# A gated four-layer stack on one core: cross attention in double steps, local heads turned later, and weight loads in another order

## The chip, the cores and the metric

One Trainium2 chip, one core of it. The metric is the time of one execution on the device in microseconds; the runs of the kernel before gave a median of 3140.57 us.

## The reference, cut to what matters

The whole program takes 2 sequences of 1024 tokens of width 256 (2048 tokens, held as 16 tiles of 128) through four layers of gated attention and gated feed-forward blocks. Two parts of it matter here.

The cross attention of layer 1 (16 heads of 64, keys from a context of 154 tokens), without its layer norm:

```python
q = (xn @ w_q).reshape(B, SQ, H, DH)
k, v = jnp.split(context @ w_kv, 2, axis=-1)
p = softmax(q @ k.T * DH ** -0.5)
x = x + tanh(g) * tanh(gate) * ((p @ v) @ w_out + b_out)
```

The local block of layer 2, run twice (DEPTH = 2), each time windowed attention (8 heads of 64, windows of 128 that look one window back) and then a gated feed-forward network:

```python
x1, x2 = split(h, 2); h = concat([x1, shift(x2, 1)])
q, k, v = split(h @ wqkv, 3)
q, k = l2norm(q) * q_scale, l2norm(k) * k_scale
q, k = rotary_xpos(q, k)
y = y + local_attention(q, k, v) @ wo
h = layernorm(shift_token(y)) * g + b
a, gate = split(h @ w1 + b1, 2)
y = y + (a * gelu(gate)) @ w2 + b2
```

Products in full precision are made of three passes over an "upper" and a "rest" part of each factor (`three`, `products`).

## The kernel before, in words

`gated_layers` runs the blocks one after the other. Each block is a function that hands each engine its own list of instructions, written out by hand in the order of the Python loops, with semaphores between the engines; nothing reorders them. Every `with nc.Block()` ends in a barrier of all engines, the small ones in `Weights` too: `Weights.__init__` issues the DMA of a pack of weights on SyncE, and `need()` makes SyncE wait until it landed, which holds all engines at the barrier.

**Cross attention** (`cross_attention`, second half, L1221 on). The unit of work u is one group of 512 tokens (4 tiles) by 4 heads: 4 groups by 4 quads, 16 units. A step n is one tile of a unit, 4 steps to a unit (64 in all). For a step TensorE makes the scores into one of two pairs of PSUM banks, VectorE takes the row's least (`largest`, L1411; the scores are negated), ScalarE four exponentials with their sums (`exps`, L1355), VectorE inverts the sums (`invert`, L1416), GpSimd multiplies (L1391), TensorE turns the probabilities two steps later (`turn_probs`), VectorE copies them out (`take_turned`, L1423), and with the last tile also the tails (L1426). For each unit TensorE also makes the queries of the next one in two halves (`project_q`, bank `QB`), which ScalarE and VectorE copy out in an upper and a rest part (`take_q` L1345, `rest_q` L1430), and the weighted values of the unit before in two halves (`weighted`, L1301 and L1305, bank `OB`), copied out the same way (`take_o` L1365, `rest_o`, recorded at the helper's line L164). After each fourth unit the output projection (`project_out`) runs in two halves through the same bank `OB`, and `add_y` (L1444) adds it to x. So `QB` and `OB` hold one item each, and the second half of a unit's weighted values waits until the first was copied out.

**Local heads** (`local_heads`), once per layer and sequence, four times in all, 8 tiles each. TensorE makes q, k and v of a tile (`qkv`, 18 matmuls), ScalarE squares q and k (L1718), VectorE sums the squares (L1749) and makes the products with the rotation tables (L1759 to L1761) and, once ScalarE took the roots (L1734), clamps and inverts them (L1764, L1766); GpSimd adds the two products (L1794) and multiplies by the inverse (L1798). One tile later TensorE turns the result (`turn_heads`, L1693), and ScalarE (L1725, L1728) and VectorE (L1771, L164) copy it out. `c_part` and `s_part` have two slots each.

**Local attention** (`local_attend`): two steps per tile (4 heads each); ScalarE and VectorE copy out the turned probabilities (`take_own` L1901, `take_prev` L1946) and each second step the weighted values (`take_o` L1907, `rest_o` L164).

**Local feed-forward** (`local_ffn`): `w.need()`, then `shifted_norm`, then `feed_forward`. Of the pack `L2f` the norm uses only the gain and shift, in ScalarE's last pass (L1582). For the second layer the packs are issued in the order L2r, L2a (the attention's, needed after the feed-forward) and L2f (the feed-forward's own).

## Time and profile before

| what | us |
|---|---|
| runs, median of 3 (lowest to highest) | 3140.57 (3138.81 to 3149.53) |
| the profiled execution, its own time | 3145.08 |
| its span, first to last instruction | 3143.3 |
| cross attention, main loop, in the span | about 985 to 1283 |
| the four runs of local heads | start at 1865.0, 2013.2, 2327.3 and 2477.7 |
| local heads, first run | 1864.9 to 1935 |
| local attention behind it | 1935 to 2011 |
| feed-forward 1 of layer 2: first load issued, norm starts | 2160.77, 2177.34 |
| feed-forward 2 of layer 2: load issued, norm starts | 2628.35, 2637.18 |

The profile is of one execution. A timeline row has start, duration, engine, line, operation, what it writes from what it reads, how many instructions it merges, and in brackets how long the engine had been idle before it and what released it. PE is TensorE, PEld its weight loads, DVE VectorE, ACT ScalarE, POOL GpSimd, SPq the queue of SyncE. The kernel is a long chain of blocks with barriers between them, so a block that ends earlier moves all that follows.

### The profile page before, as it was taken

What the parts mean: (1) busy time and instruction counts of PE and PEld (TensorE: products, weight loads), DVE (VectorE), ACT (ScalarE), POOL (GpSimd) and SP (SyncE); (2) the same over time, 40 slices, a digit from 0 to 9 for tenths busy, and PEclk for the clock granted to TensorE, in tenths of its full rate; (3) what the DMA queues carried; (4) which work ended last, traced back from release to release, by engine and by line L of the source; (5) the groups of instructions that cost most, each with busy time, mean ns of one, the idle gap of its engine ahead of it and who ended that gap; (6) DMA issues with size and microseconds to landing.
All of it is one profiled execution on the core that took longest, in us unless ns stands there. A gap on an engine that the chain in (4) does not pass through costs nothing. (4 is left out here: it accounts for less than half of the span.)

```text
span 3143.3 us, 42991 instructions
## 1 busy us (share of the span) xinstructions
PE 2438.3 (78%) x15657; PEld 1661.7 (53%) x15716; DVE 2007.2 (64%) x4265; ACT 1253.9 (40%) x2974; POOL 937.5 (30%) x867
## 2 busy tenths in 40 slices
PE   6799999979997898499997757775977776961254
PEld 3233333347876665378884446654866665850122
DVE  4588888725666555467764446565556565569898
ACT  4366666623434444143331115453334453320121
POOL 2000000004544333055550015351434442422343
PEclk9799999988998999789997679998988987985566
DMA  1111111010000000200000010001000000010000
GB/s 68 22 29 29 28 28 27 20 63 1 1 21 36 1 1 1 104 1 1 1 1 24 1 45 1 1 1 76 1 1 1 1 1 30 1 41 0 0 1 27
DMA packets 15681, 57.90 MB, mean 18 GB/s; under 512 B 7408, under 2 KB 7408, under 8 KB 13552
## 3 DMA queue, kind: packets, MB, share of 16 engines
q1 hardware_dynamic: 15472, 55.15, 5.3%
q8 instruction: 126, 2.06, 0.3%
q14 instruction: 83, 0.68, 0.1%
HBM read 39.37 MB, written 2.10 MB: 13 GB/s over the span
## 5 line engine op out<-in xcount | busy, mean ns | idle before, releaser
L2267 ACT ACTIVATE probs<-psum 128x512 f32<-128x512 f32 (+1 forms) x640 | 346.7, 593 | 195.8 <-PE psum L2211 194.9
L2282 DVE TENSOR_REDUCE max_parts<-psum 128x1 f32<-128x512 f32 x512 | 328.7, 685 | 63.2 <-PE psum L2184 59.5
L152 PE MATMUL psum<-x_upper,weights_upper 128*128 128x512 f32 (+2 forms) x624 | 252.9, 405 | 26.0 <-POOL weights_rest L164 17.0
L152 PE MATMUL psum<-x_rest,weights_upper 128*128 128x512 f32 (+2 forms) x624 | 249.7, 400 | 0.0
L152 PE MATMUL psum<-x_upper,weights_rest 128*128 128x512 f32 (+2 forms) x624 | 247.3, 396 | 0.0
L152 PE MATMUL psum<-weights_upper,hidden_upper 128*128 128x256 f32 (+2 forms) x768 | 242.3, 316 | 1.8 <-DVE x_tok L311 1.7
L164 POOL TENSOR_TENSOR weights_rest<-L1f,weights_upper 128x256 fp32r<-128x256 f32 x216 | 181.4, 866 | 183.8 <-ACT weights_upper L269 183.8
L152 PE MATMUL psum<-weights_upper,hidden_rest 128*128 128x256 f32 (+2 forms) x768 | 217.4, 283 | 0.0
L152 PE MATMUL psum<-weights_rest,hidden_upper 128*128 128x256 f32 (+2 forms) x768 | 217.2, 283 | 0.0
L2222 PE MATMUL psum<-probs,v_tok 128*17 128x256 f32 (+1 forms) x2560 | 201.1, 385 | 0.4 <-ACT probs L2267 0.4
L2211 PE MATMUL psum<-q_stack,k_stack 98*128 98x512 bf16 (+1 forms) x640 | 198.2, 387 | 0.5
L2432 POOL MEMSET selectors<- 128x2048 bf16 x1 | 1.8, 1805 | 611.1 <-DVEq L2429 611.1
L164 DVE TENSOR_TENSOR hidden_rest<-hidden,hidden_upper 128x512 fp32r<-128x512 f32 x192 | 170.3, 887 | 6.6
L2184 PE MATMUL psum<-k_stack,q_stack 96*128 96x512 bf16 x512 | 160.3, 393 | 14.9 <-DMA k_stack<-k_parts 14.9
L1921 POOL TENSOR_TENSOR probs<-probs,row_sum 128x1024 f32<-128x1024 f32 x64 | 120.9, 1894 | 165.6 <-DVE row_sum L1940 165.6
L1893 ACT ACTIVATE probs<-probs,row_least 128x256 f32<-128x256 f32 x256 | 126.9, 497 | 87.2 <-DVE row_least L1934 87.2
L164 POOL TENSOR_TENSOR weights_rest<-L2f,weights_upper 128x256 fp32r<-128x256 f32 (+1 forms) x144 | 101.6, 735 | 193.9 <-ACT weights_upper L269 193.9
L152 PEld LDWEIGHTS psum<-weights_upper,hidden_upper 128*128 128x128 f32 (+2 forms) x768 | 147.5, 192 | 12.9 <-issue 6.7
L152 PEld LDWEIGHTS psum<-weights_rest,hidden_upper 128*128 128x128 f32 (+2 forms) x768 | 146.8, 191 | 4.6
L164 POOL TENSOR_TENSOR weights_rest<-L0f,weights_upper 128x256 fp32r<-128x256 f32 x128 | 106.1, 849 | 141.7 <-ACT weights_upper L269 141.7
L152 PEld LDWEIGHTS psum<-weights_upper,hidden_rest 128*128 128x128 f32 (+2 forms) x768 | 146.5, 191 | 0.0
L152 PEld LDWEIGHTS psum<-x_upper,weights_upper 128*128 128x128 f32 (+2 forms) x624 | 117.9, 189 | 50.8 <-issue 18.1
(432 smaller groups left out, 6075.7 us busy)
## 6 DMA issues: line engine op xcount, KB each, us to landing
L1f<-in_L1f SPq DMA_DIRECT2D x1, 7936.0 KB, 21.5
k_stack<-k_parts SPq DMA_DIRECT2D x192, 36.8 KB, 2.0
q_stack<-q_parts SPq DMA_DIRECT2D x192, 32.0 KB, 2.0
L0f<-in_L0f SPq DMA_DIRECT2D x1, 4760.0 KB, 14.2
L2f<-in_L2f SPq DMA_DIRECT2D x2, 2268.0 KB, 11.6
L1x<-in_L1x SPq DMA_DIRECT2D x1, 4226.0 KB, 13.0
L2a<-in_L2a SPq DMA_DIRECT2D x2, 2048.0 KB, 10.0
L3f<-in_L3f SPq DMA_DIRECT2D x1, 3072.0 KB, 10.4
```

Source lines behind the costliest of these rows:

```text
L152: ins = pe.matmul(out, lhsT(a).bitcast(F32R), rhs(b).bitcast(F32R), start=start and n == 0, stop=stop and n == len(PASSES) - 1, skip_group ...
L164: return engine.tensor_tensor(dst.bitcast(F32R), src, up_part, ALU.subtract)
L1893: ins = act.activation(pb[:, n % NPB, h, :], pb[:, n % NPB, h, :], ACT.Exp, bias=mn[:, n % NPB, h:h + 1], scale=-1.0, accum_out=sm[:, n % ...
L1921: pool.tensor_tensor(pb[:, n % NPB], pb[:, n % NPB], spread(sm[:, n % NPB, :], 2 * P), ALU.mult)\
L2184: pe.matmul(net.ps[:, XB + (2 * n + k) % 3, :], lhsT, ks[0:ROWS, s, k * 512:(k + 1) * 512], start=True, stop=True).then_inc(x_done, 1)
L2211: pe.matmul(net.ps[0:m, STB + hf, :], ks[0:ROWS + 2, s, k * P:k * P + m], qs[0:ROWS + 2, s, hf * 512:(hf + 1) * 512], start=True, stop=True)\
L2222: ins = pe.matmul(net.ps[32 * j:32 * j + HD + 1, PVB + u % 2, 0:256], vt[0:m, b, k, h, :], pb[0:m, n % NPB, j * 256:(j + 1) * 256], start= ...
L2267: act.activation(pb[0:m, s % NPB, hf * 512:(hf + 1) * 512], net.ps[0:m, STB + hf, :], ACT.Exp, scale=HD ** -0.5).then_inc(exp_done, 1)
L2282: v.tensor_reduce(mx3[:, u % 2, q, k:k + 1], net.ps[:, XB + (2 * n + k) % 3, :], AX.X, ALU.max).then_inc(x_taken, 1)
L2432: pool.memset(sel[:], 0.0)
```

## The change: what it does

Five edits.

1. Cross attention: the banks `QB` and `OB` become a ring of two banks that all items (halves of queries, of weighted values, of projections) enter in the order of the list `ring`; an item waits until the one two places earlier was copied out (`enter`). One counter `made`, one `item_upper` and one `taken` replace those of each kind.
2. Cross attention goes in double steps: two steps' scores, a turn, the query half, (a projection half), a turn, and each second time both halves of the weighted values together. ScalarE does two steps' exponentials in a row and copies both halves of the weighted values at the head of a unit; VectorE's order follows. `exps` gets four slots, the query pair three half slots, the tails one slot.
3. Local heads: tiles are turned two tiles later (`LAG`), with a third slot of `c_part`; `s_part` keeps two and gets a wait of its own on `added`.
4. Local attention: ScalarE copies the turned probabilities before the weighted values, and VectorE too.
5. Local feed-forward: `need()` comes behind the norm, whose ScalarE waits for the pack before its last pass. In the second layer L2f is issued first, then L2a, then L2r.

```diff
-            NE, NPB = 3, 2
+            NE, NPB = 4, 2
             U = G * QUADS
-            N = U * GT
-            SLOT, TB, TAILB, OB, QB = 0, 4, 5, 6, 7
+            DU = 2 * U
+            SLOT, TB, TAILB, RING = 0, 4, 5, 6
...
-            tT = net.sb(ctx, "tailsT", [P, 2, GN])
-            qT = two(ctx, "q_pair", [P, 2, 2, GN])
+            tT = net.sb(ctx, "tailsT", [P, GN])
+            qT = two(ctx, "q_pair", [P, 3, GN])
...
+            y_unit = lambda u: u >= 2 and (u - 2) % QUADS == QUADS - 1
+            ring = [("q", 0, 0), ("q", 0, 1)]
+            for u in range(U + 2):
+                for d in range(2):
+                    if u + 1 < U:
+                        ring.append(("q", u + 1, d))
+                    if y_unit(u):
+                        ring.append(("y", group(u - 2), d))
+                    if d == 1 and 1 <= u <= U:
+                        ring += [("o", u - 1, 0), ("o", u - 1, 1)]
+            place = {item: n for n, item in enumerate(ring)}
+            uppers = {item: n for n, item in enumerate(i for i in ring if i[0] != "y")}
+            qslot = lambda u, a: (2 * u + a) % 3
+            bank = lambda item: net.ps[:, RING + place[item] % 2, :]
...
+                def enter(item):
+                    if place[item] >= 2:
+                        pe.wait_ge(taken, place[item] - 1)
...
-                    i, g, hp = 2 * u + a, group(u), (u % QUADS) * 2 + a
-                    if i >= 1:
-                        pe.wait_ge(q_ready, i)
+                    g, hp = group(u), (u % QUADS) * 2 + a
+                    enter(("q", u, a))
...
-                        ins = three(pe, net.ps[:, QB, :], [p[:, c, hp * P:(hp + 1) * P] for p in wq],
+                        ins = three(pe, bank(("q", u, a)), [p[:, c, hp * P:(hp + 1) * P] for p in wq],
...
                     pe.wait_ge(tails_taken, u + 1)
-                    if i >= 1:
-                        pe.wait_ge(o_taken, i)
-                    if y_items(u + 2):
-                        pe.wait_ge(y_taken, y_items(u + 2))
+                    enter(("o", u, a))
+                    out = bank(("o", u, a))
...
                 pe.wait_ge(cleared, 1)
                 for a in range(2):
                     project_q(0, a)
-                for n in range(N + 2 * GT):
-                    u, j = divmod(n, GT)
-                    if n < N:
-                        scores(n)
-                    if j % 2 == 0 and u + 1 < U:
-                        project_q(u + 1, j // 2)
-                    if j < 2 and y_due(u):
-                        project_out(u, j)
-                    if 2 <= n < N + 2:
-                        turn_probs(n - 2)
-                    if j >= 2 and 1 <= u <= U:
-                        weighted(u - 1, j - 2)
+                for u in range(U + 2):
+                    for d in range(2):
+                        for j in (2 * d, 2 * d + 1):
+                            if u < U:
+                                scores(u * GT + j)
+                        before = u * GT + 2 * d - 2
+                        if 0 <= before < U * GT:
+                            turn_probs(before)
+                        if u + 1 < U:
+                            project_q(u + 1, d)
+                        if y_unit(u):
+                            project_out(group(u - 2), d)
+                        if 0 <= before < U * GT:
+                            turn_probs(before + 1)
+                        if d == 1 and 1 <= u <= U:
+                            weighted(u - 1, 0)
+                            weighted(u - 1, 1)
...
-                    i = 2 * u + a
-                    act.wait_ge(pv_done, i + 1)
-                    if u % QUADS == 0 and a == 0 and u > 0:
-                        act.wait_ge(projected, y_items(u + 2))
-                    act.copy(oT[0][:, (u % QUADS) * 2 + a, :].bitcast(F32R), net.ps[:, OB, :]).then_inc(o_upper, 1)
+                    act.wait_ge(made, place["o", u, a] + 1)
+                    act.copy(oT[0][:, (u % QUADS) * 2 + a, :].bitcast(F32R), bank(("o", u, a))).then_inc(item_upper, 1)
...
-                for n in range(N + 2 * GT):
-                    u, j = divmod(n, GT)
-                    if j == 3 and 1 <= u <= U:
-                        take_o(u - 1, 0)
-                    if j == 0 and 2 <= u <= U + 1:
-                        take_o(u - 2, 1)
-                    if n < N:
-                        exps(n)
-                    if j % 2 == 0 and u + 1 < U:
-                        take_q(u + 1, j // 2)
+                for u in range(U + 2):
+                    for d in range(2):
+                        if d == 0 and 2 <= u <= U + 1:
+                            take_o(u - 2, 0)
+                            take_o(u - 2, 1)
+                        for j in (2 * d, 2 * d + 1):
+                            if u < U:
+                                exps(u * GT + j)
+                        if u + 1 < U:
+                            if d == 1:
+                                act.wait_ge(s_done, 2 * GT * (u + 1))
+                            take_q(u + 1, d)
...
+                        if u >= 1:
+                            v.wait_ge(made, place["o", u - 1, 1] + 1)
+                        v.tensor_copy(tT[:], net.ps[:, TAILB, :]).then_inc(tails_taken, 1)
...
-                for n in range(N + 2 * GT):
-                    u, j = divmod(n, GT)
-                    if n < N:
-                        largest(n)
-                    if 1 <= n <= N:
-                        invert(n - 1)
-                    if j % 2 == 1 and u + 1 < U:
-                        rest_q(u + 1, j // 2)
-                    if j == 3 and 1 <= u <= U:
-                        rest_o(u - 1, 0)
-                    if j == 0 and 2 <= u <= U + 1:
-                        rest_o(u - 2, 1)
-                    if 2 <= n < N + 2:
-                        take_turned(n - 2)
-                    if j < 2 and y_due(u):
-                        add_y(u, j)
-                    if j == 2 and u % QUADS == 1 and group(u) + 1 < G:
-                        g = group(u) + 1
-                        if g >= 2:
-                            v.wait_ge(q_made, 2 * QUADS * (g - 1))
-                        upper(v, xg[0][:, g % 2], whole_x(g)).then_inc(x_upper, 1)
+                for u in range(U + 2):
+                    for d in range(2):
+                        n = u * GT + 2 * d
+                        if n < U * GT:
+                            largest(n)
+                        if d == 0 and 2 <= u <= U + 1:
+                            rest_o(u - 2, 0)
+                        if n < U * GT:
+                            largest(n + 1)
+                        if d == 0 and 2 <= u <= U + 1:
+                            rest_o(u - 2, 1)
+                        if 2 <= n < U * GT + 2:
+                            take_turned(n - 2)
+                        if n < U * GT:
+                            invert(n)
+                        if 2 <= n < U * GT + 2:
+                            take_turned(n - 1)
+                        if u + 1 < U:
+                            rest_q(u + 1, d)
+                        if y_unit(u):
+                            add_y(group(u - 2), d)
+                        if n < U * GT:
+                            invert(n + 1)
+                        if d == 1 and u % QUADS == 1 and group(u) + 1 < G:
+                            g = group(u) + 1
+                            if g >= 2:
+                                v.wait_ge(made, place["q", (g - 1) * QUADS - 1, 1] + 1)
+                            upper(v, xg[0][:, g % 2], whole_x(g)).then_inc(x_upper, 1)
...
+            act.wait_ge(after.landed, 16)
...
-    NB = 2
+    NB, NSP, LAG = 3, 2, 2
...
-        s_part = net.sb(ctx, "sin_part", [P, NB, 2, HD])
...
-            for t in range(WIN + 1):
+            for t in range(WIN + LAG):
                 if t < WIN:
                     qkv(t)
-                if t >= 1:
-                    turn_heads(t - 1)
+                if t >= LAG:
+                    turn_heads(t - LAG)
...
-                if t >= 1:
-                    k = t - 1
+                if t >= LAG:
+                    k = t - LAG
...
+                if t >= NSP:
+                    v.wait_ge(added, t - NSP + 1)
...
-                    sp_ = s_part[:, t % NB, n].rearrange("p (h d) -> p h d", d=LD)
+                    sp_ = s_part[:, t % NSP, n].rearrange("p (h d) -> p h d", d=LD)
...
-                if t >= 1:
-                    take_rest(t - 1)
+                if t >= LAG:
+                    take_rest(t - LAG)
...
                     exps(n)
+                if 2 <= n < N + 2:
+                    take_own(n - 2)
                 if n >= 4 and n % 2 == 0 and (n - 4) // 2 < WIN:
                     take_o((n - 4) // 2)
-                if 2 <= n < N + 2:
-                    take_own(n - 2)
...
                     invert(n - 1)
+                if 2 <= n < N + 2:
+                    take_prev(n - 2)
                 if n >= 4 and n % 2 == 0 and (n - 4) // 2 < WIN:
                     rest_o((n - 4) // 2)
-                if 2 <= n < N + 2:
-                    take_prev(n - 2)
...
+        shifted_norm(net, y, hT, w("gain"), w("shift"), w)
         w.need()
-        shifted_norm(net, y, hT, w("gain"), w("shift"))
...
+        if load:
+            self.load()
+
+    def load(self):
+        with self.net.nc.Block() as block:
             @block.sync
             def _(sp):
-                sp.dma_start(memory[:], dram).then_inc(self.landed, 16)
+                sp.dma_start(self.memory[:], self.dram).then_inc(self.landed, 16)
...
-                lw = LocalWeights(net, sub, 1)
+                lw = LocalWeights(net, sub, 1, load=False)
                 with ExitStack() as ffn:
-                    local_ffn(net, y, Weights(net, ffn, "L2f0"))
+                    w = Weights(net, ffn, "L2f0")
+                    lw.pack.load()
+                    lw.rot.load()
+                    local_ffn(net, y, w)
```

**VectorE in cross attention, one unit in the middle.** Before (one unit without a projection; probsT is `take_turned`, tailsT its tails, oT_rest `rest_o`, row_least `largest`, row_sum `invert`):

```order
L1423 COPY probsT<-psum 128x4x128
L1411 TENSOR_REDUCE row_least<-psum 128x4
L1416 RECIPROCAL row_sum<-row_sum 128x4
L1430 SCALAR_TENSOR_TENSOR q_pair_rest<-psum,q_pair_upper 128x512
L164 TENSOR_TENSOR oT_rest<-psum,oT_upper 128x512
L1423 COPY probsT<-psum 128x4x128
L1411 TENSOR_REDUCE row_least<-psum 128x4
L1416 RECIPROCAL row_sum<-row_sum 128x4
L164 TENSOR_TENSOR oT_rest<-psum,oT_upper 128x512
L1423 COPY probsT<-psum 128x4x128
L1411 TENSOR_REDUCE row_least<-psum 128x4
L1416 RECIPROCAL row_sum<-row_sum 128x4
```

The change:

```order
L1419 TENSOR_REDUCE row_least<-psum 128x4 x2
L1431 COPY probsT<-psum 128x4x128
L1424 RECIPROCAL row_sum<-row_sum 128x4
L1431 COPY probsT<-psum 128x4x128
L1440 SCALAR_TENSOR_TENSOR q_pair_rest<-psum,q_pair_upper 128x512
L1424 RECIPROCAL row_sum<-row_sum 128x4
L1419 TENSOR_REDUCE row_least<-psum 128x4
L164 TENSOR_TENSOR oT_rest<-psum,oT_upper 128x512
L1419 TENSOR_REDUCE row_least<-psum 128x4
L164 TENSOR_TENSOR oT_rest<-psum,oT_upper 128x512
L1431 COPY probsT<-psum 128x4x128
L1424 RECIPROCAL row_sum<-row_sum 128x4
```

Two row_least now stand in a row, both oT_rest stand at the head of the unit, each behind one row_least, and each pair of probsT has a row_sum between them.

**ScalarE at the head of a local heads run** (squares are of tile 0, 1, 2; qT_upper and keysT_upper copy out a turned tile). Before:

```order
L1718 ACTIVATE squares<-psum 128x1024
L1732 COPY values<-psum 128x512
L1734 ACTIVATE norms<-norms 128x16
L1718 ACTIVATE squares<-psum 128x1024
L1725 ACTIVATE qT_upper<-psum 128x4x128
L1728 CAST keysT_upper<-psum 128x4x128
L1732 COPY values<-psum 128x512
L1734 ACTIVATE norms<-norms 128x16
L1718 ACTIVATE squares<-psum 128x1024
```

The change:

```order
L1735 ACTIVATE squares<-psum 128x1024
L1749 COPY values<-psum 128x512
L1751 ACTIVATE norms<-norms 128x16
L1735 ACTIVATE squares<-psum 128x1024
L1749 COPY values<-psum 128x512
L1751 ACTIVATE norms<-norms 128x16
L1735 ACTIVATE squares<-psum 128x1024
L1742 ACTIVATE qT_upper<-psum 128x4x128
L1745 CAST keysT_upper<-psum 128x4x128
```

The first copies of a turned tile have moved from behind the second squares to behind the third; TensorE's first turn has moved in the same way, from ahead of the third tile's 18 matmuls to behind them.

## Rows read from the trace of the kernel before

**Rows 1.** Stretches: length, busy us (xcount) of PE PEld DVE ACT POOL, PEclk, DMA share, GB/s

```profile
985.00:1285.00 300.00, 257.89 (x1918) 180.31 (x1916) 151.42 (x283) 137.84 (x577) 105.04 (x136) 0.98 0.01 3
1865.00:1935.00 70.00, 49.53 (x224) 39.91 (x224) 47.89 (x94) 24.42 (x44) 34.20 (x16) 0.87 0.00 1
```

**Rows 2.** Waits in 985:1285: us in total, times, longest us

```profile
PE psum L1301 <- DVE oT_rest L164: 25.9, 16, 1.7
```

**Rows 3.** Timeline of VectorE in cross attention: tails of units 0, 5, 6, 15, last add

```profile
1005.70 0.68 DVE L1426 COPY tailsT<-psum 128x512 f32<-128x512 f32 x1
...
1090.41 0.68 DVE L1426 COPY tailsT<-psum 128x512 f32<-128x512 f32 x1
...
1105.00 0.68 DVE L1426 COPY tailsT<-psum 128x512 f32<-128x512 f32 x1
...
1261.30 0.68 DVE L1426 COPY tailsT<-psum 128x512 f32<-128x512 f32 x1
...
1281.64 0.75 DVE L1444 SCALAR_TENSOR_TENSOR x_tok<-psum,cross_factor,x_tok 128x512 f32<-128x512 f32 x1 [6.02 <-PE psum L1089]
```

**Rows 4.** Timeline of all engines in cross attention, start of unit 6

```profile
1084.50 0.19 PEld L1272 LDWEIGHTS psum<-keys_upper,q_pair_upper 64*128 64x128 f32 x2 [0.81 <-issue]
...
1085.33 0.19 PEld L1089 LDWEIGHTS psum<-x_group_upper,wq_upper 128*128 128x128 f32 x1
...
1086.31 0.39 ACT L1355 ACTIVATE exps<-psum,row_least 128x154 f32<-128x154 f32 x1 [1.11 <-DVE row_least L1411]
...
1086.84 0.60 PE L1287 MATMUL psum<-const,probs 128*128 128x128 f32 x4
...
1087.79 0.61 ACT L1345 ACTIVATE q_pair_upper<-psum 128x512 fp32r<-128x512 f32 x1
...
1092.09 1.08 PE L1301 MATMUL psum<-probsT,values 128*64 128x512 f32 x4
...
1093.95 0.19 PEld L1272 LDWEIGHTS psum<-keys_upper,q_pair_upper 64*128 64x128 f32 x2 [0.81 <-ACT exps L1355]
```

**Rows 5.** Timeline of VectorE in local heads: first run, last two rows third run

```profile
1880.03 1.22 DVE L1749 TENSOR_REDUCE norms<-squares 128x16 f32<-128x1024 f32 x1
...
1890.73 1.22 DVE L1749 TENSOR_REDUCE norms<-squares 128x16 f32<-128x1024 f32 x1 [1.74 <-ACT squares L1718]
...
1895.90 1.21 DVE L1749 TENSOR_REDUCE norms<-squares 128x16 f32<-128x1024 f32 x1
...
1914.57 1.15 DVE L1764 TENSOR_SCALAR norms<-norms 128x16 f32<-128x16 f32 x1 [1.36 <-ACT norms L1734]
...
1923.05 1.22 DVE L1749 TENSOR_REDUCE norms<-squares 128x16 f32<-128x1024 f32 x1 [0.69 <-ACT squares L1718]
...
1934.25 0.69 DVE L164 TENSOR_TENSOR keysT_rest<-psum,keysT_upper 128x512 fp32r<-128x512 f32 x1
...
2351.31 1.22 DVE L1749 TENSOR_REDUCE norms<-squares 128x16 f32<-128x1024 f32 x1 [1.90 <-ACT squares L1718]
...
2387.22 1.21 DVE L1749 TENSOR_REDUCE norms<-squares 128x16 f32<-128x1024 f32 x1
```

**Rows 6.** Timeline of ScalarE and TensorE in local attention, an even step

```profile
1968.82 0.56 ACT L1907 CAST oT_upper<-psum 128x512 fp32r<-128x512 f32 x1
...
1970.81 1.09 PE L1864 MATMUL psum<-probsT,values 128*64 128x128 f32 x16 [1.55 <-DVE probsT L1946]
```

**Rows 7.** Timeline of the first local feed-forward: loads, norm's start, ScalarE's last pass

```profile
2160.77 0.33 SPq L2365 DMA_DIRECT2D L2r<-in_L2r  x1
2161.49 0.33 SPq L2365 DMA_DIRECT2D L2a<-in_L2a  x1
...
2177.44 0.22 DVE L1539 MEMSET stats<- 128x192 f32 x1 [17.82 <-PEq L2368]
...
2188.47 0.78 ACT L1582 ACTIVATE hT<-psum,L2f 128x512 f32<-128x512 f32 x1 [2.76 <-PE psum L1527]
```

**Rows 8.** DMA issues in 2625:2640: line, form, KB, us from issue to landing

```profile
L2f<-in_L2f SPq DMA_DIRECT2D x1, 2268.0 KB, 8.4
```

More of the change, by code:

```diff
@@ L1599, in __init__ @@
         self.pack_scope = ctx.enter_context(ExitStack())
-        self.pack = Weights(net, self.pack_scope, f"L2a{layer}")
+        self.pack = Weights(net, self.pack_scope, f"L2a{layer}", load)
     def split(self, net):
@@ L1711, in _ @@
                         .then_inc(h_upper, 1)
-            for t in range(WIN + 1):
+            for t in range(WIN + LAG):
                 if t < WIN:
```

89 lines of the change are left out of this document (38 added, 51 removed).

## Prediction

> **What bounds the kernel now.** I read the stretches first, then the waits of the stretch in question, then the timeline. In cross attention's main loop TensorE is busy 257.9 of 300 us at a granted clock of 0.98, with VectorE, ScalarE and GpSimd at half or less [rows 1]: TensorE is the bound there, and what can be won is its idle time. The waits name the largest piece: 16 times, once a unit, it waits up to 1.7 us for VectorE's copy of the first half of the weighted values, 25.9 us in all [rows 2]. A unit takes 14.59 us from tails to tails [rows 3]. In the first local heads run no engine is full: TensorE 49.5, VectorE 47.9 of 70 us [rows 1]. VectorE's timeline tells why: a tile begins with L1749, and the starts are 10.7 us apart from tile 1 to 2, then 5.17 us to tile 3 with no idle time noted, and 27.15 us for the four tiles to tile 7 [rows 5]. So a tile costs VectorE 5.17 us, and the rest is waiting on a loop through GpSimd and the turn. In the third run the five tiles from 2 to 7 take 35.91 us [rows 5]. In the first feed-forward of layer 2's local block the norm starts 16.7 us after the first load was issued, and ScalarE touches the pack only 11.0 us after that [rows 7].
>
> **The change part by part.** *Loads.* Before, the norm starts at 2177.44. Now it starts when three loads are issued, 0.72 us apart [rows 7]: 2160.77 + 3 x 0.72 = 2162.9, 14.5 us earlier. ScalarE's last pass would come at 2162.9 + 11.0 = 2173.9. L2f, now first on SyncE's queue, needs 8.4 us alone [rows 8], so it is there by 2169.2, 4.7 us ahead; if the three packs shared the engines evenly, they would land where they do now, just before 2177.4, and 3.5 us of the gain were lost. L2a and L2r land beside the norm and are wanted 160 us later. The second feed-forward has one load: 8.4 us from issue to landing less one empty step of 0.72 gives 7.7. `need()` stays as a block of its own, now exposed: 0.72 twice. Sum: 14.5 + 7.7 - 1.4 = **21 us off** (between 17 and 23).
>
> *Local heads.* Before, tile 2's matmuls wait behind the first turn, which waits for GpSimd. Now they follow tile 1 at once (their bank is free once VectorE made tile 0's products, before L1749 of tile 1 at 1880.03 [rows 5]). Two thirds of a tile's matmuls (about 2.8 us of its 5) and the squares put L1749 of tile 2 at 1884.4 instead of 1890.7. From there VectorE is the bound. I take 5.4 us a tile rather than 5.17, since TensorE's tile and turn fill almost as much. Tile 7 starts at 1884.4 + 5 x 5.4 = 1911.4 instead of 1923.05: 11.7 less. Behind it, a tail of 11.2 us to the last copy [rows 5] stays. The layout repeats in the second run. In the third, 4.4 + 27 = 31.4 us from tile 1 to 7 replace 10.7 (taken from the first run) + 35.9 = 46.6, 15.2 less, and the fourth I take alike. Sum: 2 x 11.7 + 2 x 15.2 = **54 us off**. At 5.17 a tile it is 58; at 6.0, 42; if only the start is won, 6.3 x 4 = 25.
>
> The third slot costs nothing: the wait for the turn of tile t-3 is over by then. `s_part` waits for GpSimd's sum of tile t-2, a tile old. ScalarE's root of tile t now stands behind copies of tile t-2, which wait for a turn that itself waits for VectorE's last copy; by the chain (a turn's first half 0.5, two copies and the values 1.5, the root 0.2, hand-overs 0.4) it is ready 2.7 us into VectorE's tile, and is wanted at 3.7.
>
> The clamp L1764 at 1914.57 took 1.15 us for 16 columns [rows 5]; it ran while GpSimd was at its sum, and reaches GpSimd more often now that GpSimd's 4.3 us a tile (34.2 us over 8 [rows 1]) must fit in 5.4 rather than 6.5. As the order stands, the clamp comes right behind the products, ahead of GpSimd's next sum. The Trainium skill, page "SBUF — State Buffer", section "Who interferes with whom", says that a tensor_scalar in a two-port mode and a GpSimd instruction exclude each other for the whole instruction, whoever issues first. By that rule the sum keeps its 54 us only as long as the clamp issues first; otherwise it is the rival on the clamp below.
>
> *Cross attention.* TensorE's own work in a unit: a step's scores 0.83, a query half 1.5, a turn 0.63 (these two from the remaining starts), half of the weighted values 1.86 [rows 4]: 4 x 0.83 + 2 x 1.5 + 4 x 0.63 + 2 x 1.86 = 12.6 of 14.6 us. The ring takes the 1.7 us away. What comes late next I step through from a unit's head, with 0.98 us from scores to exponentials, 1.48 for a step's exponentials [rows 4], and VectorE's copies at 0.6 to 0.68 [rows 3]. VectorE now does row_least, oT_rest, row_least, oT_rest before the first probsT, and has it done at 4.3; TensorE could turn the next at 3.8: 0.5 lost. The first query half waits 0.15 for oT_rest. The first probsT of the second double step stands behind two row_least: 0.35 lost. The second half of the weighted values shares a bank with the query half just made, whose copy stands on ScalarE behind two steps' exponentials, 2.96 us: 0.45 lost. Sum 1.45, so 14.1 us a unit, 0.45 less; 15 times, 6.5 us. A projection half enters between and keeps its length. The first unit has no weighted values to cover its query copy: the next unit's scores wait for both steps' exponentials, and I add 3 us. At the end, 20.3 us lie between the last tails and the last add [rows 3]; both halves of the weighted values and both of the projection now run without waiting for a copy of their bank: 1.7 + 1.1, and 2 more in the last units, which have no queries: 5 off. Sum: **8.5 us off**. Ends: TensorE without waits, 12.9 a unit, 15 x 1.7 = 25 off; 15.1 a unit, 8 more.
>
> *Local attention.* In even steps `take_own` goes ahead of `take_o`. The weighted values that follow at 1970.81 [rows 6] need both. VectorE's last copy then comes at the end of the same two copies of ScalarE, with its other copy already done: about 0.14 us less, 7 times a run; in the last even step 0.4 more. Four runs: **2 us off** (6 off to 4 on).
>
> **Sum.** 21 + 54 + 8.5 + 2 = 85.5 us off. On the profiled execution, 3145.1 - 85.5 = 3059.6; it lies 4.5 us above the median, so **3055 us** against 3140.6.
>
> **The rivals.** *Cross attention wins it all*: the waits I stepped through are in TensorE's queue slack; 17 us more off, 3038. For: the engines behind are half idle. Against: each is a real wait for a copy.
>
> *Cross attention loses a little*: double steps make each copy later; 8 us on instead of 8.5 off, 3072. For: three new waits of my own count. Against: 1.7 us are gone for certain.
>
> *Local heads keep their two speeds*: rest_out at the end of VectorE's tile holds the turn, the turn holds ScalarE's copies; only the starts are won, 29 us fewer, 3084. For: the turn still has one pair of banks. Against: the turn now has GpSimd's result a tile ahead, and that wait was the one seen.
>
> *The clamp waits for GpSimd*: if the root comes later than 3.7 us into the tile, GpSimd's sum has begun, and the clamp waits up to 2.4 us (the larger part of GpSimd's 4.3): 7.6 us a tile, 2 us on per run instead of 13.5 off, 62 us fewer, 3117. The page on SBUF, cited above, would make it so if GpSimd issued first. Against: a tile with the root in time shows VectorE's 5.17.
>
> *Slower, cross attention in series*: if a double step's probabilities must be through all engines before TensorE has anything to turn, it lasts 1.7 (scores) + 1.0 + 0.8 (row_least) + 3.0 (exponentials) + 0.3 + 2.8 (GpSimd) + 1.3 (turns) + 0.7 = 11.6 us, 23.2 a unit instead of 14.6: 16 x 8.6 = 138 on, less the other 77: 3201. It decides above 19.4 us a unit (14.6 + 77/16). Against: the turns of a double step are those of the double step before, so TensorE has half a unit of cover, 4 us and more.
>
> *The change doesn't do what it says*: the three packs land together and the norm's ScalarE waits: 3.5 us, within the range.
>
> **Numbers.** Forecast (3047 to 3064) 0.40; cross attention wins it all 0.15; loses a little 0.19; heads keep two speeds 0.14; the clamp 0.06; series 0.03; 0.03 for a mixture near no change (clamp and a small loss together with noise). The range runs from 3032 (heads at 5.17 and cross attention at 12.9) to 3090 (two speeds, with some of the loss) and leaves out about 0.15. A measurement of this kernel can tell 0.3%, 9.4 us, from no change. Faster by more: 0.94; within 0.03; slower 0.03.
>
> **What would show it.** In the profile of the changed kernel: the norms of layer 2's feed-forwards start right behind the issues, and ScalarE's L1582 group waits for TensorE, not for a DMA. Local heads: starts of the norms' reduction 5.2 to 5.5 us apart from tile 2 on, and the clamp at 0.17 us. Cross attention: tails 14.1 us apart, and the wait of the weighted values for oT_rest gone, with q_pair_rest in its place at some 0.5. Wrong would be: units above 14.6, a heads cadence that still alternates, clamps of over 1 us, or a ScalarE wait for L2f.

## The result and the profile after

The changed kernel takes **3063.58 us** (median of 4 runs, 3062.59 to 3064.13). The kernel before took 3139.69 us beside it; the ratio is 0.9752, with a 95% interval of 0.973 to 0.9774. Forecast were 3055, within 3032 to 3090. The profiled execution took 3064.06 us, its span is 3062.2 us and the mean granted clock 0.875 (before 0.876).

Stretches, in us, from the two profiled executions. Local heads are counted from the first clearing of hT to the first masked scores of the attention, local attention from there to the next block's first event.

| stretch | before | after | forecast |
|---|---|---|---|
| cross attention, last addition at | 1281.64 | 1272.43, 9.2 less | 8.5 less |
| four runs of local heads | 289.3 | 235.0, 54.3 less | 54 less |
| four runs of local attention | 307.5 | 311.7, 4.2 more | 2 less |
| two feed-forwards with their loads | 323.8 | 301.7, 22.1 less | 21 less |
| whole time | 3145.08 | 3064.06, 81.0 less | 85.5 less |

Cross attention, VectorE's timeline: the tails of units 0, 5, 6 and 15 and the last addition (for [rows 3]).

```profile
1008.45 0.68 DVE L1436 COPY tailsT<-psum 128x512 f32<-128x512 f32 x1
...
1090.38 0.68 DVE L1436 COPY tailsT<-psum 128x512 f32<-128x512 f32 x1
...
1104.55 0.68 DVE L1436 COPY tailsT<-psum 128x512 f32<-128x512 f32 x1
...
1254.84 0.68 DVE L1436 COPY tailsT<-psum 128x512 f32<-128x512 f32 x1
...
1272.43 0.75 DVE L1453 SCALAR_TENSOR_TENSOR x_tok<-psum,cross_factor,x_tok 128x512 f32<-128x512 f32 x1 [4.94 <-PE psum L1089]
```

A unit takes 14.17 us (1104.55 less 1090.38) where it took 14.59. Its waits, in 975:1275 (us in total, times, longest), for [rows 2]:

```profile
PE psum L1299 <- DVE probsT L1431: 12.5, 22, 2.1
...
PE psum L1311 <- DVE q_pair_rest L1440: 8.2, 14, 1.5
...
PE psum L1089 <- DVE oT_rest L164: 3.5, 14, 1.5
```

The 25.9 us for `oT_rest` are gone. In their place stand three smaller waits, the three that the prediction had stepped through, 24.2 us together.

Local heads, second run: the starts of VectorE's reduction for tiles 0 to 3, then a clamp and the GpSimd instruction beside it (for [rows 5]).

```profile
2001.82 1.22 DVE L1766 TENSOR_REDUCE norms<-squares 128x16 f32<-128x1024 f32 x1 [5.70 <-ACT squares L1735]
2006.05 1.22 DVE L1766 TENSOR_REDUCE norms<-squares 128x16 f32<-128x1024 f32 x1
...
2010.27 1.16 DVE L1766 TENSOR_REDUCE norms<-squares 128x16 f32<-128x1024 f32 x1
2015.74 1.21 DVE L1766 TENSOR_REDUCE norms<-squares 128x16 f32<-128x1024 f32 x1
...
2034.88 0.17 DVE L1783 TENSOR_SCALAR norms<-norms 128x16 f32<-128x16 f32 x1
2035.05 2.40 POOL L1813 TENSOR_TENSOR cos_part<-cos_part,sin_part 128x1024 f32<-128x1024 f32 x1 [0.78 <-DVE sin_part L1780]
```

From tile 3 on the starts are 5.16 us apart (tile 7 starts at 2036.39). There the clamp takes 0.17 us and comes just ahead of GpSimd's sum; only in tiles 1 and 2 of each run does it take some 0.5 us.

Feed-forward 1 of layer 2 (for [rows 7]): the issues, the start of the norm, ScalarE's first pass over the pack.

```profile
2127.61 0.33 SPq L2388 DMA_DIRECT2D L2f<-in_L2f  x1
2128.34 0.33 SPq L2388 DMA_DIRECT2D L2a<-in_L2a  x1
2129.05 0.33 SPq L2388 DMA_DIRECT2D L2r<-in_L2r  x1
2129.90 0.22 DVE L1555 MEMSET stats<- 128x192 f32 x1 [3.43 <-PEq L2385]
...
2140.99 0.78 ACT L1599 ACTIVATE hT<-psum,L2f 128x512 f32<-128x512 f32 x1 [2.83 <-PE psum L1543]
```

The norm starts 2.3 us after the first issue instead of 16.7. ScalarE waits there for TensorE, not for a DMA.

### The profile page after: what moved, and what is told of

Same layout as the page of the kernel before. It is cut to its first block and busy times, and to the rows that moved or that the text cites. A ratio compares the mean times of both kernels' runs of the same rounds, so it can differ in the third digit from the quotient of the medians.

```text
span 3062.2 us, 43018 instructions
## 1 busy us (share of the span) xinstructions
PE 2434.4 (79%) x15716; PEld 1660.0 (54%) x15716; DVE 2003.3 (65%) x4265; ACT 1250.3 (41%) x2974; POOL 937.4 (31%) x867
## 5 line engine op out<-in xcount | busy, mean ns | idle before, releaser
L152 PE MATMUL psum<-x_upper,weights_upper 128*128 128x512 f32 (+2 forms) x624 | 253.1, 406 | 26.6 <-POOL weights_rest L164 17.6
L152 PEld LDWEIGHTS psum<-weights_upper,hidden_upper 128*128 128x128 f32 (+2 forms) x768 | 147.7, 192 | 12.8 <-issue 6.7
## 6 DMA issues: line engine op xcount, KB each, us to landing
L0f<-in_L0f SPq DMA_DIRECT2D x1, 4760.0 KB, 14.3
L1x<-in_L1x SPq DMA_DIRECT2D x1, 4226.0 KB, 13.1
```

The source lines that it names most:

```text
L152: ins = pe.matmul(out, lhsT(a).bitcast(F32R), rhs(b).bitcast(F32R), start=start and n == 0, stop=stop and n == len(PASSES) - 1, skip_group ...
```

## The experiments

### The four parts alone

Each is the kernel before with one part of the change: the new `local_heads`; the loads (`need`, the order of issues, the norm's wait); the new `cross_attention`; the order of the copies in `local_attend`, of which the cut below shows ScalarE's half (VectorE's `take_prev` and `rest_o` change places in the same way).

```
 kernel before, p1_heads          kernel before, p4_attend
-NB = 2                           -take_o((n - 4) // 2)
+NB, NSP, LAG = 3, 2, 2            take_own(n - 2)
...                               +take_o((n - 4) // 2)
```

> The kernel before with the new local heads alone. Theory: the four heads stretches lose 54 us as in the changed kernel, and the local attention stretches behind them grow by 1 to 1.8 us each although their own order is the old one, because TensorE comes out of the heads at the lower clock; so 48 to 51 us off in all. Rival (the new order of copies is what made local attention longer): attention stretches stay at 76.2 to 78.0 us and 54 us are off.

Measured: 3100.39 us, ratio 0.9864 (0.9849 to 0.9879), 42.4 off where 48 to 51 were expected. Heads 234.4 us in all, 54.8 less than in the trace before. Local attention 313.7 us, 6.2 more, **with the old order of copies**.

> The kernel before with the new loads and the norm's wait alone. Theory: 22 us off, 14.3 in the first feed-forward and 7.8 in the second, independent of the rest. Rival (part of it depends on the earlier end of the blocks ahead): under 18 us off.

Measured: 3126.90 us, 0.9951 (0.9935 to 0.9968). The feed-forwards are 13.7 and 7.5 us shorter, 21.2 in all. By the medians only 15.9 us are off, on the rival's side of 18. But the two stretches lost what the theory said, so the difference lies in stretches that this edit doesn't touch, such as the old cross loop, which ended 4.1 us later here than in the trace before.

> The kernel before with the new cross attention alone. Theory: 9 us off, units of 14.17 us. Rival (another stage pays for it through the clock): 9 us off inside the loop, less at the end of the program.

Measured: 3133.01 us, 0.9965 (0.995 to 0.9979). Units of 14.17 us, last addition at 1271.59.

> The kernel before with the new order of copies in local attention alone. Theory: pairs of steps 8.88 instead of 8.96 us, a few tenths lost at each run's end, so 0 to 2 us off, which timing can hardly tell from nothing. Rival (the order itself costs the 4.2 us by which the attention stretches grew): 3 to 5 us on.

Measured: 3140.76 us, 0.9994 (0.9984 to 1.0003). Local attention 307.1 us against 307.5.

What follows: the order of copies is worth nothing either way, and the attention's growth comes with the new heads. The four medians lie 42.4, 15.9, 9.8 and 2.0 us under the 3142.77 us of before in that series, 70 in all, where the whole change lies 76 under the kernel before in its own series (3139.69). The traces show part of why. The old code does not take the same time in every execution: the old cross loop ended at 1285.22, 1285.74 and 1282.62 in the traces with the heads, the loads and the order of copies alone, and at 1281.64 in the one read for the forecast. The old heads took 289.3 us in that one, but 287.1, 283.8 and 283.1 in the traces with the loads, the cross attention and the order of copies alone. Against 283 us the new heads win 49 and not 55, and with 6 to 7 us given back in the attention that is the 42.4 of the first run.

### TensorE's clock at the start of the attention

The granted clock of short stretches shows what the new heads do to the attention behind them. First before, then after, the fourth run: the 5 us from the first masked scores, and the next 5 (length, busy us of PE, PEld, DVE, ACT, POOL, PEclk, DMA share, GB/s).

```profile
2550.34:2555.34 5.00, 2.84 (x25) 2.35 (x23) 4.51 (x26) 4.53 (x19) 1.99 (x2) 0.72 0.02 3
2555.34:2560.34 5.00, 5.00 (x41) 4.28 (x42) 2.25 (x10) 3.97 (x16) 2.62 (x2) 0.66 0.00 0
```

```profile
2475.16:2480.16 5.00, 2.93 (x25) 2.34 (x23) 4.49 (x26) 4.53 (x19) 1.98 (x2) 0.50 0.00 0
2480.16:2485.16 5.00, 5.00 (x36) 4.45 (x36) 2.11 (x10) 2.89 (x12) 1.77 (x1) 0.50 0.00 0
```

0.50 is the lower level, 1.2 GHz. Run by run the attention grew by 1.1, 0.1, 1.8 and 1.2 us, and the second run, which did not grow, is the one where the clock reads as before. Its first 5 us, before and after:

```profile
2083.75:2088.75 5.00, 2.38 (x25) 1.88 (x23) 4.46 (x26) 4.53 (x19) 1.99 (x2) 0.82 0.01 2
```

```profile
2050.49:2055.49 5.00, 2.27 (x25) 1.77 (x23) 4.46 (x26) 4.53 (x19) 1.99 (x2) 0.84 0.00 2
```

In the new heads TensorE ends its projections early: it then has one group of eight transpositions left after 4.1 us of waiting and another after 1.5 us, and these already take 1.92 and 1.94 us where in mid-run they take 1.06 (second run, timeline after):

```profile
2041.79 1.92 PE L1710 MATMUL psum<-const,cos_part 128*128 128x128 f32 x8 [4.10 <-DVE keysT_rest L164]
...
2045.19 1.94 PE L1710 MATMUL psum<-const,cos_part 128*128 128x128 f32 x8 [1.49 <-DVE keysT_rest L164]
```

The kernel before ends its heads at the lower level too: its last group waits 5.17 us and takes 1.97 (first run).

```profile
1931.63 1.97 PE L1693 MATMUL psum<-const,cos_part 128*128 128x128 f32 x8 [5.17 <-POOL cos_part L1798]
```

What differs is how soon the clock comes back: there within the first 5 us of the attention, if not yet for good, after the change not before 10 us in three runs of four. Why it comes back later is not shown. The test keeps TensorE at work with matmuls whose results nobody reads:

```
+idle(14)                # 14 matmuls, 512 columns, free banks
 turn_heads(WIN - 2)
+idle(8)
 turn_heads(WIN - 1)
+idle(8)
...
 scores(2)               # in the attention: only in the second of these two kernels
+7 matmuls of 512 columns
 turn_probs(0)
```

> The changed kernel, with TensorE kept busy at the end of the local heads: 14 extra matmuls of 512 columns ahead of turning tile 6, 8 ahead of turning tile 7, 8 behind it, all into banks that nobody reads afterwards. Theory (the local attention is longer because TensorE enters it at 1.2 GHz, after about 4 us without work in the tail of the heads): the two last groups of eight turns take 1.1 us instead of 1.92, the tail of each run of heads is 1 to 1.5 us shorter, each stretch of local attention 1 to 1.5 us shorter and near the 76.2 to 78.0 us of the kernel before; in all 8 to 11 us, about 3054. Rival (something else at the start of the attention costs the time, e.g. what ScalarE and VectorE do there): stretches of attention stay at 77.1 to 79.2 us, and the extra matmuls cost nothing or hold up the turns by up to 1 us a run: 3063 to 3068.

Measured: 3048.62 us, 0.9703 (0.9688 to 0.9717). Heads 225.7 us, 9.3 less than after. Attention 310.2, only 1.5 less where 4 to 6 were expected.

> As the run before, and 7 more extra matmuls in the attention, ahead of its first transposition of probabilities, where TensorE waited 2.45 us for GpSimd. Theory: the first turned probabilities take 1.1 instead of 1.97 us, 1 us less a run than with the heads' extra matmuls alone: about 3050. Rival: the same time as the run before, or up to 1 us a run more, since the extra matmuls hold up that transposition.

Measured: 3044.02 us, 0.9686 (0.9672 to 0.9701), where 3050 was expected. Attention 302.7 us, 9.1 less than after and 7.5 less than in the run before, not 4. Heads 229.8, 4.1 more than in the run before: three of their four runs begin at a clock of 0.50 here, two there.

The same two windows of the fourth run, of the first and then of the second kernel:

```profile
2464.59:2469.59 5.00, 1.69 (x25) 1.27 (x21) 4.46 (x26) 4.76 (x20) 1.99 (x2) 0.85 0.00 0
2469.59:2474.59 5.00, 5.00 (x36) 4.45 (x36) 2.11 (x10) 2.89 (x12) 1.76 (x1) 0.50 0.01 3
```

```profile
2461.98:2466.98 5.00, 3.49 (x32) 2.51 (x28) 4.46 (x26) 4.76 (x20) 1.99 (x2) 1.00 0.01 3
2466.98:2471.98 5.00, 4.96 (x56) 4.07 (x56) 2.94 (x11) 4.46 (x17) 3.10 (x2) 1.00 0.00 0
```

So the clock is the cause of the attention's 4.2 us, and the theory was right on that and wrong on the place. Warm heads alone bring TensorE into the attention at 2.4 GHz, but it loses that again while it waits for GpSimd's first probabilities: the second window reads 0.50 in this fourth run and 0.66 in the other three. In those three the first output addition comes 24.5 us into the attention as in the kernel before (24.7), in this one at 25.4 as after the change, and with both waits filled at 23.1 in all four. Only with work in that wait too does the clock stay up, and the attention falls to 4.9 us less than in the kernel before.

### The clamp behind GpSimd's start

```
 ins.then_inc(parts, 1)          # GpSimd's sum may start
-v.wait_ge(sd_ready, t + 1)
-clamp, reciprocal
...
 take_rest(t - LAG)
+v.wait_ge(sd_ready, t + 1)
+clamp, reciprocal
```

> The changed kernel with the clamp and the reciprocal of the norms moved behind the taking of the tile before last, so that GpSimd's sum of 2.35 us has been running for about 1.3 us when the clamp comes. If the clamp must wait for a running GpSimd instruction: it takes about 1.1 us instead of 0.16 wherever it follows a taking, VectorE (which has some 0.1 us a tile to spare) falls behind by about 0.8 us a tile, 24 tiles: near 3080. If there is no such wait in this place: the clamp takes 0.16 us, 3063, within 0.2%.

Measured: 3083.89 us, 0.9815 (0.9799 to 0.9832), 20.3 us over the changed kernel; heads 257.6 us, 22.6 more. VectorE's group, then one tile of GpSimd and VectorE:

```profile
L1785 DVE TENSOR_SCALAR norms<-norms 128x16 f32<-128x16 f32 x32 | 36.4, 1137 | 0.0
```

```profile
2029.50 2.36 POOL L1817 TENSOR_TENSOR cos_part<-cos_part,sin_part 128x1024 f32<-128x1024 f32 x1 [1.62 <-DVE sin_part L1780]
...
2030.54 1.35 DVE L1785 TENSOR_SCALAR norms<-norms 128x16 f32<-128x16 f32 x1
```

The clamp begins 1.04 us into the sum and ends at 2031.89, with the sum (2031.86). The clamp of [rows 5] did the same in the kernel before: it ended at 1915.72, GpSimd's sum at 1915.68. So the rival on the clamp is a real mechanism. It didn't come because the root is ready in time and the clamp issues ahead of the sum. By the rule of the Trainium skill, page "SBUF — State Buffer", section "Who interferes with whom", which the prediction weighed, it is the one that issues first that keeps the other out; the trace agrees, 0.17 us when the clamp is first, 1.35 when the sum is.

### Slots or lag

```
-NB, NSP, LAG = 3, 2, 2
+NB, NSP, LAG = 3, 2, 1
```

> The changed kernel with three slots in the heads' cosine buffer, but turned one tile later, as before, instead of two. Theory (the lag is what took TensorE's wait for GpSimd away; slots alone only let VectorE run ahead): heads of 69 to 72 us instead of 58.7, 3063.6 plus 40 to 54, near 3110. Rival (VectorE's wait for a free slot was the tie): heads below 62 us, under 3075.

Measured: 3106.36 us, 0.9883 (0.9866 to 0.99); heads 283.8 us, as in the other traces with the old heads (283.1 to 289.3). TensorE's wait in the first run of heads is back, to the tenth what it was in the kernel before (second row):

```profile
PE psum L1710 <- POOL cos_part L1817: 17.6, 7, 5.2
```

```profile
PE psum L1693 <- POOL cos_part L1798: 17.6, 7, 5.2
```

It is the lag that gives the gain; the third slot alone gives nothing. Whether the lag would do without the third slot was not run. In this run local attention takes 307.1 us, so the old heads also bring back the old attention.

### Cross attention: the ring and the double steps

```
 for j in (2 * d, 2 * d + 1):
+    if u + 1 < U and j == 3:
+        act.wait_ge(s_done, 2 * GT * (u + 1))
+        take_q(u + 1, 1)
     exps(u * GT + j)
-if d == 1: ...take_q(u + 1, 1)
```

> The changed kernel, with ScalarE taking the unit's second projection between the third and the fourth list of exponentials instead of behind both (its wait for the scores still ahead of it). Theory (the unit of 14.17 us holds a wait of TensorE in front of the second weighted half for q_pair_rest, 14 times 0.58 us, because that projection is taken late): the wait L1311<-q_pair_rest goes, 0.4 us in each of 15 units, 5 to 6 us in all, about 3058. Rival: the fourth list of exponentials is now 0.6 us late, and what hangs on it (the reciprocal, GpSimd's share, the first scores of the next unit) takes the gain back: 3063, or up to 5 us more.

Measured: 3055.81 us, 0.9722 (0.9708 to 0.9737), 7.8 less than the changed kernel. Units of 13.54 and 13.78 us, last addition at 1263.72, 8.7 us earlier: 5 of it in the units and their end, as expected, and 3.7 in the first unit, whose tails now come at 1004.78. The fourth list's lateness took nothing back.

The next run keeps before's single steps and changes the banks. With them one copy moves: in the units with a projection VectorE takes the first query half ahead of the first addition, so that the ring's order holds.

```
-SLOT, TB, TAILB, OB, QB = 0, 4, 5, 6, 7
+SLOT, TB, TAILB, RING = 0, 4, 5, 6
+bank = lambda item: net.ps[:, RING + place[item] % 2, :]
```

> The changed kernel, with the cross attention of before in its single steps and its order, but with the ring of two banks in place of one bank for projections and one for outputs (in the units with a y, VectorE's taking of the first projection moved ahead of the first addition, so that the ring's order holds). Theory: the ring takes away the wait of the second weighted half for the first half's copy (25.9 us, 16 times 1.6), the double steps save little by themselves: last addition 6 to 9 us earlier than before's 1281.64, 3063 to 3067. Rival: it is the double steps that carry the gain, since in single steps the second half stands behind the copy of the projection instead: 3070 to 3074.

Measured: **3050.07 us**, 0.9704 (0.9684 to 0.9724), 13.5 less than the changed kernel. The theory said 3063 to 3067, the rival 3070 to 3074; both fell. Tails and the last addition:

```profile
1004.65 0.68 DVE L1431 COPY tailsT<-psum 128x512 f32<-128x512 f32 x1
...
1085.97 0.68 DVE L1431 COPY tailsT<-psum 128x512 f32<-128x512 f32 x1
...
1099.82 0.68 DVE L1431 COPY tailsT<-psum 128x512 f32<-128x512 f32 x1
...
1261.40 0.75 DVE L1449 SCALAR_TENSOR_TENSOR x_tok<-psum,cross_factor,x_tok 128x512 f32<-128x512 f32 x1 [4.85 <-PE psum L1089]
```

The tails are those of units 0, 5 and 6. A unit takes 13.85 us, the last addition comes 20.2 us earlier than before, and 11.0 earlier than after. So the ring alone is worth 20 us, and **the double steps, with their copies as ordered in this change, cost 11**. The first tails come at 1004.65 instead of 1008.45: 3.8 us in the first unit, where by the code the first query copy need no longer wait for both steps' exponentials. The next fourteen units take 229.0 instead of 231.8 us, and the last is 10.3 instead of 14.6; these last 4 us are the least certain, since in the traces of the run with a lag of 1 and of the first kernel of the next section, both in double steps, that unit took 10.7 too. Nor are the 11 us a price of double steps as such. The run with the early taking stays in double steps and won 8.7 us by the place of one copy of ScalarE, and the same loop in the first kernel of the next section ended at 1259.99, 1.4 us ahead of this one. TensorE's wait for `probsT` ahead of its turns (12.5 us after the change) is 1.4 us here, once. The largest that is left, in 975:1275:

```profile
PE psum L1311 <- DVE q_pair_rest L1435: 13.7, 14, 1.0
```

### A version that beats both

Two kernels put the pieces together. The first has the double steps with the early taking, and TensorE's extra matmuls at the end of the heads, in the attention and ahead of each run of heads:

```
+pe.wait_ge(qkv_upper, 3)        # while the weights are split
+20 matmuls of 512 columns
...
+6, 8 and 3 matmuls              # in the tail of local attention
```

> The changed kernel with three things together: ScalarE takes the second projection early in the cross attention; TensorE kept busy with extra matmuls at the end of the heads and ahead of the attention's first transposition; and, new, extra matmuls ahead of each run of heads too (20 while the local weights are split, 17 in three places of the tail of each local attention), since in the run with both warmings the heads still began at a granted clock of 0.50 where they took 58 us and at 1.00 where they took 55. From the run with both warmings (3044.0): minus 7.8 for the early taking, minus 3 for each of four runs of heads: 3024, if the pieces add up and the clock at the start of the heads is what separates 58 from 55. Rival: the start of the heads isn't set by the clock (VectorE and ScalarE move the first tiles): 3036. By either theory it is faster than both kernels.

Measured: 3032.83 us, 0.9649 (0.9632 to 0.9666). The pieces did not add up: the early taking and the attention kept theirs (last addition 1259.99, attention 302.6), but the heads won 5.2 us of 12. The first 8 us of the first and the second run of heads:

```profile
1844.47:1852.47 8.00, 6.02 (x27) 4.95 (x28) 2.57 (x6) 2.05 (x4) 0.00 (x0) 0.79 0.01 2
1976.26:1984.26 8.00, 6.02 (x34) 5.10 (x35) 2.58 (x7) 3.08 (x5) 0.00 (x0) 1.00 0.01 3
```

The second run, at 1.00, took 55.02 us; the other three began at 0.79 to 0.84 and took 56.4 to 56.6. The last kernel has the ring in single steps, VectorE's second taking one step earlier, and more extra matmuls where the clock was not yet up:

```
-if j == 3: rest_q(u + 1, 1)
+if j == 2: rest_q(u + 1, 1)     # at the step's end
...
-pe.wait_ge(qkv_upper, 3), 20 matmuls
+pe.wait_ge(qkv_upper, 1), 30 matmuls
...
+6 matmuls between turn_y and qkv(0)
```

> The ring in single steps (as in the run with the ring alone), with one more edit in it: VectorE takes the second projection at the end of step 2 instead of in step 3 behind the list and the reciprocal, since the trace of the ring alone shows TensorE's only regular wait of a unit there (the second weighted half for q_pair_rest, 14 times 0.98 us). Beside it the warmings of TensorE, with 30 instead of 20 extra matmuls at the splitting of the weights, and 6 between turning y and the first projection. From the kernel with all warmings and the early taking in double steps (3032.8, last addition at 1260): if the ring in single steps plus the earlier taking shortens a unit of 13.85 us by 0.7 to 0.9 in 15 units, the last addition comes at about 1249, and the time is near 3020, with up to 4 us less from the heads' starts. Rival: the unit is bound by TensorE's own work or by the lists of exponentials, and stays at 13.85: 3031 to 3034.

Measured: **3014.82 us** (5 runs, 3013.71 to 3015.45), 0.9596 (0.9583 to 0.9609) of the kernel before, 48.8 us under the changed kernel. Units take 12.8 us, the last addition comes at 1246.77, and TensorE's window is nearly full (first row); all four runs of heads start at 1.00 (second row, the first run) and take 55.0 us.

```profile
975.00:1242.00 267.00, 254.35 (x1905) 179.22 (x1904) 156.91 (x299) 137.10 (x577) 107.38 (x137) 0.99 0.01 1
```

```profile
1831.10:1839.10 8.00, 7.42 (x40) 6.13 (x41) 2.59 (x7) 3.09 (x5) 0.00 (x0) 1.00 0.00 0
```

## Why the prediction was right or wrong

**The direction and the likeliest case** held: 3063.6 lies in the forecast's own 3047 to 3064, if at its upper edge, and three of the four parts did what the prediction said they do. The sum was 4.5 us too large on the profiled execution (85.5 against 81.0). The median missed by 8.6 us, since the execution before lay 4.5 us above its median, and the one after only 0.5. Those 4.5 us sat mostly in the old heads: with the order of copies alone the profiled execution took 3139.15 us, 5.9 less than the one before, and its heads 6.2 less. So the forecast read its savings from a trace with that excess and took them off the median, which does not hold it.

**Loads**, 21 forecast, 22.1 measured (21.2 alone). Each step held: the first norm starts 2.3 us behind the first issue, 14.4 earlier than before (14.5 forecast), L2f is there in time, and the packs that land together did not come: ScalarE has no wait for a DMA there. The stretches are 14.3 and 7.8 us shorter, so the 0.72 that the prediction charged twice for `need()` hardly shows, and that is the 1.1 us of difference.

**Local heads**, 54 forecast, 54.3 measured; by runs 12.3, 12.5, 16.2 and 13.3 where 11.7 twice and 15.2 twice stood. The two speeds are gone. In the first run tile 2 comes 19.4 us after the start, as forecast (17.9, 17.6 and 19.1 in the others), and the cadence is VectorE's 5.16, with 5.5 from tile 2 to 3, instead of the 5.4 that I took as allowance for TensorE: "TensorE's tile and turn fill almost as much" was too careful. The 58 us which that cadence was to give did not come mainly because of the fourth run's start: its tile 0 comes 10.7 us after the start, at a granted clock of 0.50, where it came after 8.0 at 1.00 in the kernel before. The tail kept its length, 14.1 us from tile 7 to the first masked scores (13.9 to 14.2 before). That the total fits is in part luck of the trace: the 15.2 us for the third and fourth runs hang on the 74.1 and 72.7 us that these took in the trace before, and in three other traces with the old heads they took 70.1 to 71.1. Against those the new heads win 48 to 49 us. That the lag, not the slots, carries it was tested, and so was the rival on the clamp.

**Local attention**, 2 less forecast, 4.2 more measured: the step that failed. The prediction read the step of the steady loop. Its pair of steps is 8.88 us instead of 8.96 in the trace after, but alone the new order gave 0.4 us in all. It did not ask at what clock TensorE comes out of the new heads. The price was paid in the next block: the attention's growth appears with the new heads alone and goes when TensorE is kept at work. That it comes from TensorE's ending early in the new heads is the likely reason, but not shown. The term was mis-sized by 6.2 us, more than the whole miss of 4.5 in the sum; the other terms gave the rest back.

**Cross attention**, 8.5 forecast, 9.2 measured, from other pieces than told. The unit of 14.1 is 14.17 and the first unit's 3 us are 2.75 (1008.45 against 1005.70). But the end won 2.7 us instead of 5 (17.6 against 20.3), and the last two units before it are 2.3 us longer (14.2 and 14.6 instead of 13.4 and 13.1). On the other side the three pairs of units with a projection won 7.3 us in all (39.4 to 39.5 each instead of 41.3, 43.0 and 41.4), where 0.45 a unit gave them 2.7. These errors nearly cancel, which is luck. The 14.1 also rests on a smaller floor than the best case does: the 1.45 us lost were added to 12.6, while the best case took 12.9 (14.6 less 1.7), by which the unit would be 14.3. A larger thing the prediction did not see, since it gave ring and double steps one price: split, it is 20 us off for the ring and 11 on for the double steps in this order of copies. Of the three waits it stepped through, it took all as what must follow once the 1.7 us are gone; the two for `probsT` belong to the double steps and are not there in single ones; they cost little, since with the early taking they stand unchanged (12.5 us, 22 times) in units of 13.5 to 13.8 us. The rival "cross attention wins it all" had units of 12.9 us. The last kernel has 12.8, in single steps and with one copy moved: TensorE's own work was the floor, as counted, but this change's order could not reach it.

## What to carry to other kernels

Price a restructuring by its parts, and run each alone: here one half of the new loop (two shared banks) was worth twice the whole, and the other half (double steps) gave half of it back, mostly by the place of one copy. After a change that lets TensorE finish early, look at the granted clock of the stretch behind it and of the next block's first microseconds; a few matmuls into free banks can be worth more than the wait they fill. A small VectorE instruction such as this clamp is cheap or dear beside a long GpSimd one by which of the two issues first (0.17 or 1.35 us), so keep it right behind the instruction that releases GpSimd, not two copies later. And before a sum is taken off one trace, look whether its stretches repeat in others: here the old heads took 283 to 289 us.

## What the runs showed that I had not expected

- Keeping TensorE busy with unread matmuls is worth 19.6 us here (3063.58 to 3044.02), though they take no work away and no wait. Where they filled the heads' end but left the attention's wait of 2.45 us open, the attention kept all but 1.5 of its 311.7 us. They help only where they reach: in the first run of that kernel the clock fell to 0.88 and then 0.54 in the last 7.5 us of the attention, and the 1.1 us won at its start were lost there.
- A run of heads with its end kept busy has a price by the clock of its start: 57.6 to 58.1 us when its first 8 us are granted 0.50, 56.1 to 56.6 at about 0.8, 55.0 at 1.00.
- The old cross loop differs from execution to execution by about 4 us at its end (1281.64, 1282.62, 1285.22, 1285.74), where the new loop mostly ends within 1.2 us (1271.24 to 1272.43 in five kernels) but came out at 1267.23 in a sixth, with a last unit of 10.7 us instead of 14.6. Why that unit has two lengths stays open.
